# A landmark-attention decoder layer in f32: the column and row sums of the second attention move to GpSimd as trees of additions, the scale of its inverse is worked out over batches 1 to 4, and two softmax divisions are moved

## The chip, the core and the metric

The kernel runs on one core of one Trainium2 chip. A core has TensorE (matrix products, written PE in the profile; its weight loads are PEld), VectorE (DVE), ScalarE (ACT), GpSimd (POOL) and SyncE (SP), which issues most of the transfers. Each engine works through its own list of instructions in order, and they wait for one another by semaphores alone. The metric is the device time of one execution in microseconds. The kernel before takes 201.53 us, the median of three runs (200.58 to 201.87).

## The reference, cut to what matters

Eight batches of 128 tokens with 128 features go through landmark attention with 16 heads, an attention over a context, and a layer of experts, each followed by a layer norm. All of it is in f32. The change touches the first of the three:

```python
q_l = q.reshape(b, H, M, l, DH).sum(axis=3) / l      # M = 32 landmarks, l = 4, scale = DH ** -0.5
k_l = k.reshape(b, H, M, l, DH).sum(axis=3) / l
attn1 = softmax(q   @ k_l^T)      # 128 x 32 for each of 8 x 16 heads
attn2 = softmax(q_l @ k_l^T)      # 32 x 32
attn3 = softmax(q_l @ k^T)        # 32 x 128
z = attn2^T / (max(attn2.sum(-1)) * max(attn2.sum(-2)))   # both maxima over all batches and heads
for _ in range(6):
    az = attn2 @ z
    z = 0.25 * z @ (13 * I - az @ (15 * I - az @ (7 * I - az)))
out = attn1 @ z @ (attn3 @ v)
out = out + conv(out)                                     # along the tokens, 13 taps
```

The factor 1 / (max * max) is one number for the whole input. It is what the iteration starts from, and so the first matrices of the iteration need it.

## The kernel before, in words

**Setup.** The weights are transposed, landmark queries and keys formed, and the second attention `A2` [128, 32 groups, 32] is computed. Its softmax ends on VectorE. For each of 16 heads TensorE then forms a landmark map from the keys' and queries' weights, and ScalarE (10 heads) and VectorE (6 heads, `GG_VECTOR`) copy it from PSUM to `GG`. VectorE also transposes `A2` in 32 x 32 blocks into `A2T`.

**The scale.** VectorE sums `A2` and `A2T` along their rows (L1084, L1086), takes the largest of each (L1088, L1089) and gives `peak_ready`. TensorE turns these columns into rows (`peaks`, L520), VectorE takes the maximum over them, multiplies and inverts (L1091 to L1096), TensorE spreads the result over the 128 partitions (`scale`, L526), and VectorE copies it out (L1118), which gives `c_ready`. GpSimd scales `A2` by it into `V` (L376). TensorE squares `A2T` in two halves (`squares`, L559), and ScalarE scales these into `V` too (`first_P`, L909).

**The batch loop.** TensorE, VectorE, ScalarE and GpSimd each run through steps s = 0, 1, ... in an order written out by hand; later stages of a batch come some steps after its first. For batch s TensorE makes the scores of the first attention (L612) and of the third (L619). VectorE takes the maxima (L1106, L1109), subtracts the first (L1112) and scales the second (L1114). ScalarE does the exponentials: `A1` in one instruction (L921), `E3` in four (L924), with their sums. One step later VectorE sums `A1` and inverts both sums (L1128 to L1132), and GpSimd multiplies `E3` and `A1` by the inverses (L381, L384). Three steps later TensorE transposes `E3` (L645) and VectorE copies it (L1124); after four, TensorE multiplies by the tokens (L652) and ScalarE copies (`YT`, L918); after five, TensorE multiplies by the values' maps `NV` (L661), and ScalarE copies the result `R` (L937), which lies in the place of `E3`.

Other work is set in between, by the step s at which it stands in each engine's list: on TensorE `peaks` and `scale` at s = 0, the small transposes of the context and of a bias (L546 to L552) at s = 0, `squares(0)` at 1, the second half of the values' maps (`head_values(1)`, L534) at 2, `squares(1)` at 3. ScalarE copies the results of the small transposes after its exponentials of batch 0 (L896 to L903), and those of `head_values(1)` after batch 1 (L889, L891). VectorE begins batch 1 by an addition that waits for one of these copies (L1101, `gsum_ready`).

**The rest.** TensorE then runs the convolution of the first attention (L593), the 24 products of the iteration (L564, L570, in a hardware loop of 8 turns), with VectorE (L1147 to L1164) and ScalarE (L949) in turns with it, the product of inverse and `R` (L703), the output projection, and after that the second and third part of the layer.

The code below is printed with the profile's line numbers.

## Time and profile before

| | us |
|---|---|
| median of 3 runs (lowest, highest) | 201.53 (200.58, 201.87) |
| the profiled execution: its own time | 203.06 |
| span from its first to its last instruction | 201.3 |
| TensorE busy | 175.7 (87%) |
| VectorE busy | 123.8 (61%) |
| ScalarE busy | 97.0 (48%) |
| GpSimd busy | 68.7 (34%) |
| granted TensorE clock, mean | 0.975 of full |

The span is in the trace's own time, and the profiled execution was 1.8 us longer than it, and 1.5 us longer than the median run. TensorE's busy time is modelled from pipelined instructions, so that a stretch in which it is fully busy says that work stood ready, and not that the array ran at its peak. A shares-of-the-span table mixes stages with different limits; the stage of this change lies between 24 and 83 us.

### The profile page before, as it was taken

The numbers are of one execution on the slowest core, as the hardware profiler recorded it, in microseconds if no ns is written. First come the engines' busy times: TensorE is split into PE (matmuls) and PEld (weight loads), VectorE is DVE, ScalarE is ACT, GpSimd is POOL, SyncE is SP. The second block draws the span as 40 slices with busy tenths as digits, with TensorE's granted clock in tenths as the row PEclk, the third lists the DMA queues.
The fourth block names the chain that finished last, engine by engine and source line by source line (L and its number), as shares of the span: only waits on it lengthen the run. The fifth ranks groups of instructions, "written<-read, shape, count | busy, mean of one in ns | idle before, by whom it ended". The sixth has DMA issues, their size and how long they took to land. (4 is left out here: it accounts for less than half of the span.)

```text
span 201.3 us, 11917 instructions
## 1 busy us (share of the span) xinstructions
PE 175.7 (87%) x5244; PEld 153.5 (76%) x5244; DVE 123.8 (61%) x363; ACT 97.0 (48%) x264; POOL 68.7 (34%) x129
## 2 busy tenths in 40 slices
PE   0998996999999999739999999999899969899940
PEld 0986884767666769639899888999799759899940
DVE  0232798499998280235899893242579803988881
ACT  2422882569787446412343343322245617566750
POOL 6180000557565300000000001810226740689884
PEclk9999999999999999985999999999999999999996
DMA  5944000000000000000000000005960858787300
GB/s 178 373 125 141 7 0 0 0 10 3 0 3 0 3 3 7 3 3 3 0 0 0 2 2 0 7 3 165 352 101 26 250 144 224 200 215 234 97 8 4
DMA packets 15632, 14.57 MB, mean 72 GB/s; under 512 B 1350, under 2 KB 12001, under 8 KB 15603
## 3 DMA queue, kind: packets, MB, share of 16 engines
q1 hardware_dynamic: 14867, 13.10, 23.1%
q0 software_dynamic: 736, 1.06, 1.5%
q8 instruction: 21, 0.34, 0.7%
q14 instruction: 8, 0.07, 0.1%
HBM read 12.08 MB, written 2.53 MB: 73 GB/s over the span
## 5 line engine op out<-in xcount | busy, mean ns | idle before, releaser
L564 PE MATMUL banks<-V 32*32 32x64 f32 x1664 | 37.6, 231 | 6.0 <-issue 4.3
L564 PEld LDWEIGHTS banks<-V 32*32 32x32 f32 x1664 | 33.7, 107 | 8.6 <-issue 7.9
L570 PE MATMUL banks<-MM,WT 32*32 32x64 f32 x1536 | 35.8, 233 | 0.0
L570 PEld LDWEIGHTS banks<-MM,WT 32*32 32x32 f32 x1536 | 30.8, 107 | 0.0
L1154 DVE SCALAR_TENSOR_TENSOR MM<-V,banks 128x512 f32<-128x512 f32 x24 | 16.5, 686 | 18.1 <-PE banks L564 17.6
L949 ACT ACTIVATE V<-banks 128x512 f32<-128x512 f32 x20 | 11.9, 597 | 24.4 <-PE banks L570 24.4
L387 POOL MEMSET WT<- 128x1950 f32 x1 | 1.7, 1723 | 57.5 <-PE banks L570 57.5
L1019 ACT ACTIVATE GG<-banks,b1T 128x128 f32<-128x128 f32 x60 | 16.9, 378 | 5.6 <-PE banks L848 5.6
L848 PE MATMUL banks<-qkl,GG 128*128 128x128 f32 x120 | 15.9, 277 | 2.5 <-DVE qkl L1400 1.8
L848 PEld LDWEIGHTS banks<-qkl,GG 128*128 128x128 f32 x120 | 14.5, 192 | 3.1 <-DVE qkl L1400 2.0
L827 PE MATMUL banks<-E,GG 128*128 x120 | 16.3, 279 | 0.5 <-ACT GG L1019 0.5
L433 POOL DMA_INDIRECT out_x<-qkl,number_u x15 | 15.4, 1026 | 3.5 <-issue 3.5
L827 PEld LDWEIGHTS banks<-E,GG 128*128 128x128 f32 x120 | 14.6, 191 | 1.0 <-issue 0.7
L381 POOL TENSOR_TENSOR E<-E,st 128x512 f32<-128x512 f32 x8 | 8.3, 1043 | 10.2 <-DVE st L1128 10.2
L924 ACT ACTIVATE E<-banks,st 128x128 f32<-128x128 f32 x32 | 11.2, 368 | 0.0
L376 POOL TENSOR_SCALAR V<-A,st 128x512 f32<-128x512 f32 x2 | 3.1, 1594 | 23.3 <-DVE st L1118 23.3
L619 PEld LDWEIGHTS banks<-xT,GG 128*128 128x128 f32 x64 | 8.2, 191 | 3.7 <-issue 2.6
L661 PEld LDWEIGHTS banks<-NV,YT 128*32 128x32 f32 x256 | 6.6, 109 | 5.3 <-issue 5.3
L424 POOL TENSOR_TENSOR st<-st 128x1 f32<-128x1 f32 x13 | 7.6, 581 | 8.6 <-DVE st L1387 8.3
L1147 DVE SCALAR_TENSOR_TENSOR GB<-V,eye_a 128x256 f32<-128x256 f32 x24 | 10.0, 418 | 0.0
L1164 DVE TENSOR_TENSOR WT<-GB,banks 128x256 f32<-128x256 f32 x24 | 9.9, 414 | 0.0
L408 POOL DMA_INDIRECT sorted_tokens<-MM,slot_u x8 | 8.4, 1056 | 4.2 <-ACT MM L970 2.2
(217 smaller groups left out, 401.0 us busy)
## 6 DMA issues: line engine op xcount, KB each, us to landing
GG<-in_L_ffn_w SPq DMA_DIRECT2D x15, 256.0 KB
wqkv<-in_L_attn_w_qkv SPq DMA_DIRECT2D x3, 512.0 KB, 5.3
Tt<-padded_taps SPq DMA_DIRECT2D x1, 1024.0 KB, 5.7
sorted_tokens<-WT SPq DMA_DIRECT2D x1, 975.0 KB, 13.5
GG<-in_L_ffn_b SPq DMA_DIRECT2D x15, 64.0 KB
WT<-sorted_tokens SPq DMA_DIRECT2D x1, 585.0 KB, 4.6
x_sb<-in_x SPq DMA_DIRECT2D x1, 512.0 KB, 4.0
wfc<-in_L_attn_w_fc SPq DMA_DIRECT2D x1, 512.0 KB, 6.9
```

Of the source, the lines that this page charges most:

```text
L408: nc.gpsimd.indirect_dma_start(out=xs_dram.ap(), out_offset=bass.IndirectOffsetOnAxis(slot_u[:, b:b + 1], 0), in_=x2e[:, b, :], in_offset= ...
L433: nc.gpsimd.indirect_dma_start(out=out.rearrange("b n d -> (b n) d"), out_offset=bass.IndirectOffsetOnAxis(number_u[:, j:j + 1], 0), in_=y ...
L564: return mm(bank[PV_BANKS[k % RING]][quad(q), 64 * n:64 * n + 64], V[quad(q), g, 0, :], V[quad(q), g], start=True, stop=True)
L570: return mm(bank[QM_BANKS[k % RING]][quad((q + 2) % 4), 64 * n:64 * n + 64], Q[quad(q), g, :], MM[quad(q), g], start=True, stop=True)
L827: i = mm(bank[4 + j % 2][:, 0:D], hT[:, j % 3, P * k:P * k + P], w2s[:, experts[j], k, :], start=(k == 0), stop=(k == FK - 1))
L848: i = mm(bank[s % 3][:, P * k:P * k + P], w1b[:, s % W1_SLOTS, P * k:P * k + P], xsT[:, s, :], start=True, stop=True)
L924: nc.scalar.activation(E3[:, s, g, :], bank[5 + s % 2][:, N * g:N * g + N], ACT.Exp, bias=stat("nm3", HG * s + g, 1), scale=DH ** -0.5 / L ...
L949: nc.scalar.mul(V[:, ring(k + CH)], ps, 0.25).then_inc(V_ready, 1)
L1019: nc.scalar.activation(hT[:, j % 3, P * k:P * k + P], bank[j % 3][:, P * k:P * k + P], ACT.Gelu, bias=b1T3[:, experts[j], k:k + 1]).then_i ...
L1147: step(v.scalar_tensor_tensor(out=GB[:, g], in0=V[:, g, 0, :], scalar=QB, in1=eye_a[:].unsqueeze(1).broadcast_to([P, GC, M]), op0=ALU.mult ...
L1154: v.scalar_tensor_tensor(out=MM[:, g].rearrange("p g w m -> p (g w m)"), in0=V[:, g].rearrange("p g w m -> p (g w m)"), scalar=ROOT, in1=p ...
L1164: v.tensor_tensor(Q[:, g, :], GB[:, g], pv[:].rearrange("p (g w m) -> p g w m", g=GC, w=2)[:, :, 0, :], ALU.add).then_inc(Q_ready, 1)
```

## The change

The sums of `A2` and `A2T` are made by GpSimd, each as a tree of five additions (widths 16, 8, 4, 2, 1) in `MM`, which is free at that time. `peaks` goes to step 2 of TensorE (1 of VectorE), `scale` to step 3 (2 and 3), `squares` to 3 and 4, both `first_P` to 4 of ScalarE, and the two scalings by GpSimd behind batches 3 and 4. VectorE stores its six landmark maps one after the other and transposes `A2` behind them. The landmark maps are stored times `SIM_SCALE`, so that the exponentials and the maximum need no factor. The third attention's division is made on `R` (`scaled_R`, eight instructions behind all batches) and not on `E3`, and both sums are inverted by one instruction. The part of the diff that carries this:

```diff
+            def sums(src, out):
+                width, terms, at = M // 2, src, 0
+                while width >= 1:
+                    total = scratch[:, at:at + GROUPS * width].rearrange("p (g m) -> p g m", g=GROUPS) if width > 1 else out
+                    add = nc.gpsimd.tensor_tensor(total, terms[:, :, 0:width], terms[:, :, width:2 * width], ALU.add)
+                    if width > 1:
+                        add.then_inc(half_sums, 1)
+                        sums_begun[0] += 1
+                        pool.wait_ge(half_sums, sums_begun[0])
+                    else:
+                        add.then_inc(sums_ready, 1)
+                    terms, at, width = total, at + GROUPS * width, width // 2
...
+            pool.wait_ge(A2_ready, 2)
+            sums(A2[:], stat("cs").unsqueeze(2))
+            pool.wait_ge(A2T_ready, 1)
+            pool.wait_ge(sums_ready, 1)
+            sums(A2T[:], stat("rows").unsqueeze(2))
...
+            def scaled_R(b):
+                pool.wait_ge(R_ready, b + 1)
+                nc.gpsimd.tensor_tensor(R[:, b], R[:, b], stat("sm", (HG + H) * b, HG).unsqueeze(2)
+                                        .broadcast_to([P, HG, N]), ALU.mult).then_inc(R_scaled, 1)
...
+                if b in (3, 4):
+                    first_W(b - 3)
+            for b in range(B):
+                scaled_R(b)
...
-                    if s == 0:
-                        peaks()
...
+                if s == 2:
+                    peaks()
+                if s == 3:
+                    scale()
                 if s == 0:
-                    scale()
                     pe.wait_ge(NV_ready, 1)
...
-                if s == 1:
-                    pe.wait_ge(A2T_ready, 1)
-                    pe.wait_ge(c_ready, 1)
-                    squares(0)
...
                 if s == 3:
+                    pe.wait_ge(b1T_ready, 1)
+                    pe.wait_ge(A2T_ready, 1)
                     pe.wait_ge(NV_ready, 2)
+                    squares(0)
+                if s == 4:
+                    pe.wait_ge(c_ready, 1)
                     squares(1)
-                    pe.wait_ge(b1T_ready, 1)
                 if 3 <= s < B + 3:
                     b = s - 3
-                    pe.wait_ge(attn3_ready, b + 1)
+                    pe.wait_ge(exp3_done, HG * (b + 1))
...
-                    if b < 2:
-                        pe.wait_ge(V_ready, 2 * (b + 1))
+                    if b == 0:
+                        pe.wait_ge(V_ready, CH)
...
-            pe.wait_ge(R_ready, B)
+            pe.wait_ge(R_scaled, B)
...
-                if s == 1:
+                if s == 2:
+                    head_values(1, 0, 4)
+                if s == 4:
                     first_P(0)
-                    head_values(1, 0, 4)
-                if s == 3:
                     first_P(1)
...
-            for h in (9, 11, 13, 15):
-                GG_copy(h)
-            step(v.tensor_reduce(stat("cs"), A2[:], AX_X, ALU.add))
-            dve.wait_ge(A2T_ready, 1)
-            step(v.tensor_reduce(stat("rows"), A2T[:], AX_X, ALU.add))
...
-                    step(v.tensor_reduce(stat("nm3", HG * s, HG),
-                                         bank[5 + s % 2][:].rearrange("p (g n) -> p g n", g=HG), AX_X, ALU.max))
+                    v.tensor_reduce(stat("nm3", HG * s, HG), bank[5 + s % 2][:].rearrange("p (g n) -> p g n", g=HG),
+                                    AX_X, ALU.max, negate=True).then_inc(max3_ready, 1)
...
-                    v.tensor_scalar(stat("nm3", HG * s, HG), stat("nm3", HG * s, HG), -DH ** -0.5 / L, None,
-                                    ALU.mult).then_inc(max3_ready, 1)
-                if s == 0:
+                if s == 1:
+                    peaks()
+                if s == 2:
+                    scale()
+                if s == 3:
                     dve.wait_ge(c_mm, 1)
...
-                    v.reciprocal(stat("r3", HG * b, HG), stat("s3", HG * b, HG)).then_inc(rsum3, 1)
                     dve.wait_ge(exp1_done, b + 1)
-                    step(v.tensor_reduce(stat("rs1", H * b, H), A1[:, b], AX_X, ALU.add))
+                    step(v.tensor_reduce(stat("sm", (HG + H) * b + HG, H), A1[:, b], AX_X, ALU.add))
```

How this stands in the engines' lists is shown at three places. Line numbers are each kernel's own. First TensorE, steps 2 and 3 of the kernel before (L534 is `head_values(1)`, L559 `squares`, L645 the first transpose of `E3`):

```order
L612 MATMUL banks<-GG,GB 128x512 [waits sim1_shift]
L619 MATMUL banks<-xT,GG 128x128 [waits exp3_done]
L619 MATMUL banks<-xT,GG 128x128 x3
L534 MATMUL banks<-wfc,WT 128x128 [waits ctxT_ready]
L534 MATMUL banks<-wfc,WT 128x128 x7
L612 MATMUL banks<-GG,GB 128x512 [waits sim1_shift]
L619 MATMUL banks<-xT,GG 128x128 [waits exp3_done]
L619 MATMUL banks<-xT,GG 128x128 x3
L559 MATMUL banks<-A2T 32x32 [waits NV_ready]
L559 MATMUL banks<-A2T 32x32 x63
L645 MATMUL banks<-ident,E 128x128 [waits attn3_ready,b1T_ready]
```

The same steps in the changed kernel (L549 is `peaks`, L563 `head_values(1)`, L555 `scale`, L588 `squares(0)`):

```order
L646 MATMUL banks<-xT,GG 128x128 [waits exp3_done]
L646 MATMUL banks<-xT,GG 128x128 x3
L549 MATMUL banks<-ident,st 1x128 [waits peak_ready]
L549 MATMUL banks<-ident,st 1x128
L563 MATMUL banks<-wfc,WT 128x128 [waits ctxT_ready]
L563 MATMUL banks<-wfc,WT 128x128 x7
L641 MATMUL banks<-GG,GB 128x512 [waits sim1_shift]
L646 MATMUL banks<-xT,GG 128x128 [waits exp3_done]
L646 MATMUL banks<-xT,GG 128x128 x3
L555 MATMUL banks<-st,ones 128x1 [waits cinv_ready,const_ready]
L588 MATMUL banks<-A2T 32x32 [waits NV_ready,A2T_ready,b1T_ready]
L588 MATMUL banks<-A2T 32x32 x63
```

`peaks` now stands ahead of `head_values(1)`, and `scale` and a first half of the squares ahead of the first transpose of `E3`; in the kernel before one half of the squares stood in step 1 already. Second, ScalarE from batch 1 on in the kernel before (L909 is `first_P`, L889 and L891 store `NV`):

```order
L921 ACTIVATE A<-A 128x512 [waits sim1_shift]
L924 ACTIVATE E,st<-banks,st 128x128 [waits max3_ready]
L924 ACTIVATE E,st<-banks,st 128x128 x3
L909 ACTIVATE V<-banks,st 128x16x32 [waits c_ready,P0_mm]
L889 COPY NV<-banks 128x4x128 [waits NV_mm]
L891 COPY NV<-banks 128x4x128
```

The same engine in the changed kernel from batch 2 on (L920, L922 store `NV`, L951 stores `YT`, L940 is `first_P`):

```order
L954 ACTIVATE A<-A 128x512 [waits sim1_shift]
L957 ACTIVATE E,st<-banks,st 128x128 [waits max3_ready]
L957 ACTIVATE E,st<-banks,st 128x128 x3
L920 COPY NV<-banks 128x4x128 [waits NV_mm]
L922 COPY NV<-banks 128x4x128
L954 ACTIVATE A<-A 128x512 [waits sim1_shift]
L957 ACTIVATE E,st<-banks,st 128x128 [waits max3_ready]
L957 ACTIVATE E,st<-banks,st 128x128 x3
L951 COPY YT<-banks 128x512 [waits YT_mm]
L954 ACTIVATE A<-A 128x512 [waits sim1_shift]
L957 ACTIVATE E,st<-banks,st 128x128 [waits max3_ready]
L957 ACTIVATE E,st<-banks,st 128x128 x3
L940 ACTIVATE V<-banks,st 128x16x32 [waits c_ready,P0_mm] x2
```

The storing of `NV` stands behind the exponentials of batch 2 and no longer behind those of batch 1, and both `first_P` behind those of batch 4. Third, GpSimd between its first additions and the batches, in the changed kernel; none of these ten rows is in the kernel before, where the two scalings by the factor stood here:

```order
L380 TENSOR_TENSOR MM<-A 128x512
L380 TENSOR_TENSOR MM<-MM 128x256
L380 TENSOR_TENSOR MM<-MM 128x128
L380 TENSOR_TENSOR MM<-MM 128x64
L380 TENSOR_TENSOR st<-MM 128x32
L380 TENSOR_TENSOR MM<-A2T 128x512
L380 TENSOR_TENSOR MM<-MM 128x256
L380 TENSOR_TENSOR MM<-MM 128x128
L380 TENSOR_TENSOR MM<-MM 128x64
L380 TENSOR_TENSOR st<-MM 128x32
```

## Rows read from the trace of the kernel before

**Rows 1.** A stretch: start:end us, length, busy us (instructions) by engine, clock, DMA share, GB/s.

```profile
50.00:55.00 5.00, 5.00 (x51) 3.14 (x50) 4.90 (x13) 3.85 (x14) 2.90 (x3) 1.00 0.00 0
```

**Rows 2.** Instructions of TensorE in time: start us, duration us, what, idle before it.

```profile
30.71 1.16 PE L534 MATMUL banks<-wfc,WT 64*128 64x128 f32 x16 [0.71 <-DVE GG L1074]
...
32.12 1.07 PE L612 MATMUL banks<-GG,GB 128*128 128x512 f32 x2
...
45.86 1.29 PE L559 MATMUL banks<-A2T 32*32 32x32 f32 x128 [0.38 <-ACT NV L891]
47.08 0.66 PE L645 MATMUL banks<-ident,E 128*128 128x128 f32 x4
47.57 1.02 PE L612 MATMUL banks<-GG,GB 128*128 128x512 f32 x2
48.43 1.05 PE L619 MATMUL banks<-xT,GG 128*128 128x128 f32 x8
```

**Rows 3.** Waits of TensorE, 24 to 84 us: total, times, longest.

```profile
PE banks L520 <- DVE st L1089: 1.2, 1, 1.2
```

**Rows 4.** Instructions of ScalarE in time.

```profile
37.51 0.63 ACT L921 ACTIVATE A<-A 128x512 f32<-128x512 f32 x1 [4.21 <-DVE A L1112]
...
39.87 0.22 ACT L902 ACTIVATE res<-banks 128x8 f32<-128x8 f32 x1
...
42.24 0.63 ACT L921 ACTIVATE A<-A 128x512 f32<-128x512 f32 x1 [2.08 <-DVE A L1112]
...
44.15 0.69 ACT L909 ACTIVATE V<-banks,st 128x512 f32<-128x512 f32 x1
...
45.18 0.62 ACT L891 COPY NV<-banks 128x512 f32<-128x512 f32 x1
```

**Rows 5.** Instructions of VectorE in time.

```profile
31.68 1.20 DVE L1084 TENSOR_REDUCE st<-A 128x32 f32<-128x1024 f32 x1
...
40.12 0.17 DVE L1101 TENSOR_TENSOR res<-res,gw 128x8 f32<-128x8 f32 x1 [2.50 <-ACT res L902]
40.20 0.68 DVE L1106 TENSOR_REDUCE st<-banks 128x16 f32<-128x512 f32 x1
...
42.13 0.16 DVE L1114 TENSOR_SCALAR st<-st 128x4 f32<-128x4 f32 x1
...
43.14 0.63 DVE L1106 TENSOR_REDUCE st<-banks 128x16 f32<-128x512 f32 x1
...
49.49 0.63 DVE L1106 TENSOR_REDUCE st<-banks 128x16 f32<-128x512 f32 x1
...
52.97 0.63 DVE L1106 TENSOR_REDUCE st<-banks 128x16 f32<-128x512 f32 x1
```

**Rows 6.** Groups of GpSimd by shape: busy us, mean ns of one, idle before.

```profile
L384 POOL TENSOR_TENSOR A<-A,st 128x512 f32<-128x512 f32 x8 | 8.4, 1050 | 0.0
L376 POOL TENSOR_SCALAR V<-A,st 128x512 f32<-128x512 f32 x2 | 3.1, 1594 | 23.3 <-DVE st L1118 23.3
L394 POOL TENSOR_SCALAR MM<-st 128x1 f32<-128x1 f32 x8 | 1.7, 210 | 0.6
```

**Rows 7.** Stretches around the start of the iteration, columns as in Rows 1.

```profile
85.00:88.00 3.00, 1.35 (x125) 1.32 (x127) 0.87 (x4) 0.11 (x2) 0.00 (x0) 1.00 0.00 0
88.00:92.00 4.00, 1.86 (x128) 1.66 (x116) 1.23 (x3) 0.58 (x1) 0.00 (x0) 0.61 0.03 8
92.00:96.00 4.00, 3.81 (x268) 3.61 (x257) 2.71 (x6) 1.19 (x2) 0.00 (x0) 0.54 0.00 0
```

**Rows 8.** VectorE in the iteration, one row of this line for each product.

```profile
92.16 0.69 DVE L1154 SCALAR_TENSOR_TENSOR MM<-V,banks 128x512 f32<-128x512 f32 x1 [2.93 <-PE banks L564]
...
94.39 0.69 DVE L1154 SCALAR_TENSOR_TENSOR MM<-V,banks 128x512 f32<-128x512 f32 x1 [0.88 <-PE banks L564]
...
99.20 0.69 DVE L1154 SCALAR_TENSOR_TENSOR MM<-V,banks 128x512 f32<-128x512 f32 x1 [0.38 <-PE banks L564]
...
103.76 0.69 DVE L1154 SCALAR_TENSOR_TENSOR MM<-V,banks 128x512 f32<-128x512 f32 x1 [0.39 <-PE banks L564]
```

More of the change, by code:

```diff
@@ L24 @@
 GROUPS = B * HG
+SIM_SCALE = DH ** -0.5 / L
 CH = 4
@@ L372, in _ @@
                                     ).then_inc(xb_ready, 1)
-            pool.wait_ge(c_ready, 1)
-            for n in range(2):
+            def sums(src, out):
[10 more added lines that the diff above has]
+                    terms, at, width = total, at + GROUPS * width, width // 2
@@ L558, in squares @@
                         t = A2T[quad(q), g, :]
-                        i = mm(bank[3 + n][quad(q), M * (g % 16):M * (g % 16) + M], t, t, start=True, stop=True)
+                        i = mm(bank[4 - n][quad(q), M * (g % 16):M * (g % 16) + M], t, t, start=True, stop=True)
                 i.then_inc(P0_mm, 1)
@@ L883, in _ @@
                 act.wait_ge(GG_mm, h + 1)
-                nc.scalar.copy(GG[:, :, :, h, :].rearrange("p b w m -> p w b m"),
-                bank[(4 + h) % 8][:].rearrange("p (w b m) -> p w b m", w=2, b=B)).then_inc(GG_scalar, 1)
+                nc.scalar.mul(GG[:, :, :, h, :].rearrange("p b w m -> p w b m"),
+                              bank[(4 + h) % 8][:].rearrange("p (w b m) -> p w b m", w=2, b=B), SIM_SCALE
+                              ).then_inc(GG_scalar, 1)
             def head_values(n, first, second):
@@ L1080, in _ @@
+            for h in GG_VECTOR:
+                GG_copy(h)
             dve.wait_ge(A2_ready, 2)
             v.transpose(A2T[:].rearrange("p g m -> p (g m)"), A2[:].rearrange("p g m -> p (g m)")).then_inc(A2T_ready, 1)
-            for h in (9, 11, 13, 15):
-                GG_copy(h)
-            step(v.tensor_reduce(stat("cs"), A2[:], AX_X, ALU.add))
-            dve.wait_ge(A2T_ready, 1)
-            step(v.tensor_reduce(stat("rows"), A2T[:], AX_X, ALU.add))
-            settle()
-            step(v.tensor_reduce(stat("peak", 0, 1), stat("cs"), AX_X, ALU.max))
@@ L1089, in _, with peaks @@
-            v.tensor_reduce(stat("peak", 1, 1), stat("rows"), AX_X, ALU.max).then_inc(peak_ready, 1)
-            dve.wait_ge(peak_mm, 1)
-            step(v.tensor_reduce(stat("pk")[0:1, :], bank[3][0:1, 0:256].rearrange("p (w n) -> p w n", w=2),
-                                 AX_X, ALU.max))
-            settle()
-            step(v.tensor_tensor(stat("prod")[0:1, :], stat("pk", 0, 1)[0:1, :], stat("pk", 1, 1)[0:1, :], ALU.mult))
-            settle()
-            v.reciprocal(stat("cinv")[0:1, :], stat("prod")[0:1, :]).then_inc(cinv_ready, 1)
+            def peaks():
+                dve.wait_ge(sums_ready, 2)
+                step(v.tensor_reduce(stat("peak", 0, 1), stat("cs"), AX_X, ALU.max))
+                settle()
+                v.tensor_reduce(stat("peak", 1, 1), stat("rows"), AX_X, ALU.max).then_inc(peak_ready, 1)
@@ new lines, in scale @@
+            def scale():
+                dve.wait_ge(peak_mm, 1)
+                step(v.tensor_reduce(stat("pk")[0:1, :], bank[3][0:1, 0:256].rearrange("p (w n) -> p w n", w=2),
+                                     AX_X, ALU.max))
+                settle()
+                step(v.tensor_tensor(stat("prod")[0:1, :], stat("pk", 0, 1)[0:1, :], stat("pk", 1, 1)[0:1, :], ALU.mult))
+                settle()
+                v.reciprocal(stat("cinv")[0:1, :], stat("prod")[0:1, :]).then_inc(cinv_ready, 1)
```

44 lines of the change are left out of this document (23 added, 21 removed).

## The prediction, written before the changed kernel ran

> **What bounds the kernel now.** I read the busy shares first. TensorE is busy in 175.7 of 201.3 us, but that is an average over stages, so the stage of the change is read by stretches. From 50 to 55 us TensorE is busy in all 5.00 us and VectorE in 4.90 [rows 1]. Both look full, and the list in time tells them apart: VectorE begins a batch every 52.97 - 49.49 = 3.48 us [rows 5], and from batch 5 on TensorE has more than that to do for each. Between the first scores at 32.12 us [rows 2] and the end of the convolution at 82.6 us, TensorE stands still at few places: 1.2 us before `peaks` [rows 3], 0.38 us before `squares(1)` [rows 2], and pauses of weight loads around `scale` and the scores of batch 3 that I put at 0.1 and 0.6 us. Everything else there is work, and the changed kernel does the same work. So the end of this stage is: the time at which the first scores start, plus the same work, plus the pauses. From there on nothing is moved but one wait, and the rest of the kernel should shift as a whole. The question is only which pauses go and which come.
>
> **The start of the stage.** VectorE no longer transposes `A2` between its landmark maps, so the maps that `head_values(0)` waits for are stored 1.15 us sooner. The pause of 0.71 us before it [rows 2] goes; the pause has no more than this in it, since TensorE's own map products end then. What stands between it and the first scores takes 32.12 - 30.71 = 1.41 us of issue. First scores: 30.00 + 1.41 = 31.41 us, **0.7 us sooner**. The last map and the moved transpose (1.2 us, as for one L1084 [rows 5]) are through at 31.9, before the scores end at 32.5. Storing the maps with a factor is taken at the price of the copies; a map costs VectorE some 0.61 us of issue, and it has some 0.7 us to spare there, so up to a tenth more on each of six would cost nothing.
>
> **Batch 0.** `peaks` and `scale` are gone from step 0, with their 1.2 and 0.1 us. The scores of the third attention follow 0.86 us behind those of the first (48.43 - 47.57 [rows 2]) and end 1.05 us later, at 33.3. VectorE needs 0.64 us for the maximum, no longer waits for its end before subtracting (0.1 us a batch), and the subtraction of 0.69 us ends at 34.7. ScalarE starts its exponentials at 34.7 where it started at 37.51 [rows 4]: 2.8 us sooner. From there to the end of the copy that VectorE waits for is 39.87 + 0.22 - 37.51 = 2.58 us [rows 4], unchanged. VectorE begins batch 1 at 37.4 where it began at 40.20 [rows 5], again 2.8 us sooner. TensorE meanwhile does the small transposes and the scores of batches 1 and 2, and is through with them at 38.0, as the pitches of the same work give it (small transposes 1.14, scores 0.86 + 0.92 a batch).
>
> **First new pause, 1.6 us.** `peaks` stands behind those scores and waits for VectorE's two small maxima, which stand behind batch 1's three instructions. These took 42.13 - 40.20 = 1.93 us [rows 5], now 0.1 less: 37.4 + 1.8 = 39.2, plus some 0.4 for the small ones. TensorE stands from 38.0 to 39.6.
>
> **Second new pause, 2.1 us.** TensorE then does `peaks`, `head_values(1)` (1.09), and batch 3's scores, to 42.9, and `scale` for which VectorE is ready at 43.0. Next come `squares(0)`, and their list has a wait for `NV`, as bank 4 is shared. ScalarE stores `NV` behind the exponentials of batch 2. VectorE begins batch 2 at 39.6 + 0.86 - 0.1 = 40.4 (sum and inverse as between 42.13 and 43.14, less 0.15 for the two small instructions removed [rows 5]), so the subtraction ends at 42.25. The exponentials take 44.15 - 42.24 = 1.91 us, and storing `NV` takes 45.18 + 0.62 - 44.15 = 1.65 less the 0.57 of `first_P`, 1.08 [rows 4]. `NV` is stored at 45.3. TensorE stands from 43.2 to 45.3.
>
> **Where that leaves TensorE.** In the kernel before it started the second half of the squares at 45.86, with the first half done. Now it starts the first half at 45.3, with the second ahead. A half costs 47.08 - 45.86 = 1.22 us [rows 2]: -0.55 + 1.22 = **+0.7 us**.
>
> **Third new pause, 0.7 us.** The first product with `NV` (L661) now waits for both `first_P`, which ScalarE has behind batch 4's exponentials, and these behind the storing of `YT`. The product by the tokens ends at 51.4; then 0.48 + 1.91 + 1.27 = 3.66 us on ScalarE give 55.1. TensorE would be free at 54.4. So another **+0.7**, together **+1.4 us**.
>
> **What is covered.** The two trees: 992 elements each. At the nearest row of two inputs, 1050 ns for 512 [rows 6], 2.0 us, and with 0.2 us for the start of each of five and as much for each wait on itself, 3.6; from below 2.0, from above, at the slowest row (1594 ns for 512) with both, 5.1. The first may start at 27.05, when `A2` is ready, the second at 31.9, and `peaks` wants them at 39.2. Up to 6.0 us a tree nothing comes of it. The two scalings of 1.6 us are wanted some 20 us after they end. The eight multiplications of `R`, 1.04 us each, end some 1.1 us after the last `R`, near 79 us, and are wanted at 126. The multiplications of `E3` held nobody. On VectorE 0.27 us a batch is saved (two small instructions and the wait for the maximum), from batch 4 on under TensorE's work: nothing. Should those be worth their full 8 x 0.27 = 2.2 us, see the first rival.
>
> **The sum.** +1.4 us on the profiled execution, whose span would be 202.7; against the median run, 201.53 + 1.4 = **202.9**. The profiled execution was 1.5 us above that median, so its successor's own time says little alone. The start of the stage is surest within 0.3 us, the pauses within 0.4: +0.7 to +2.1. That is no change: a measurement tells about 1% (2.0 us) from none. Chance **0.48**.
>
> **Rival 1: VectorE paces the batches, and the kernel is faster.** For it: VectorE is at 4.90 of 5.00 us, batch 1 begins 2.8 us sooner, and 0.27 us a batch is removed. If the pauses I lay out were shorter, because ScalarE's and VectorE's pieces overlap more than the rows show, all of the 2.8 us would reach the end: 198.7. Against it: TensorE is at 5.00 of 5.00 [rows 1], and the three pauses hang on the order of the lists, which is fixed. With the loop entry below going well in addition it could also come out just under. Chance 0.13, of which 0.1 below -1%.
>
> **Rival 2: TensorE's clock falls in the new pauses, and the kernel is slower.** In the kernel before TensorE was busy in 1.35 of 3 us from 85 to 88, and then the granted clock fell to one half, 1.2 of 2.4 GHz: means of 0.61 and 0.54 over 8 us are some 6.8 us at the lower level [rows 7]. There the pauses before the fall were of 1.9 and 2.1 us. In the changed kernel TensorE would be busy in some 3.7 of the 7.3 us from 38.0 to 45.3, much the same picture, where before it was full. What it costs: a product of the iteration took 94.39 - 92.16 = 2.23 us at the lower level and (103.76 - 99.20) / 3 = 1.52 at the full [rows 8], so a third of the time is lost. Over 6.8 us that is 2.2 us, over half that long, as TensorE has work at hand at once here, 1.1; the whole +2.5 to +3.6, 204.0 to 205.1. It decides from the first fall after 43 us. Chance 0.28.
>
> The Trainium skill, in "TensorE: Matmul & The Clock Gate", section "Why this matters for your kernels", ties a fall to one long pause between bursts of products. By that rule neither of the new pauses would bring a fall, this rival would have next to no chance, and the sum would stay at +1.4. The trace disagrees: the fall at 88.9 us had only two short pauses ahead of it, with work between them [rows 7]. So the row decides, and the chance stays.
>
> **Rival 3: the trees are late.** Short runs of 16, 8, 4 elements may cost GpSimd more than a row of 512 shows. The trace has no such shape. At 7 us a tree, `peaks` comes 1.9 us later and everything behind it: +3.3, 204.8. Chance 0.05.
>
> **Rival 4: the loop's entry comes out otherwise.** From 82.5 to 96 us, where TensorE first runs through the loop's body, it loses some 5 us to pauses without a visible cause and to the lower clock. I let it shift as it stands. If the pauses or the clock fall otherwise, the whole moves by up to 1.6 us either way. Chance 0.06, and it widens each case.
>
> **The numbers.** The forecast's own range with the entry's noise is 201.4 to 204.0. Taking in rival 2 and the near edge of rival 1: 201.0 to 205.0, outside of it about 2 in 10. Slower by over 1%: 0.23 of rival 2, 0.05, 0.02 and 0.07 of the forecast's own upper end, 0.37. Faster by over 1%: 0.10 and 0.01, 0.11. The rest, 0.52, within 1%.
>
> **What would show it.** In the changed kernel's list: first scores near 31.4; ScalarE's first exponential near 34.7; a pause of TensorE before L549 ended by VectorE, near 1.6 us; one before L588 ended by `NV`, near 2.1; squares starting near 45.3; one before the first product with `NV`, ended by `V`, 0.7; the convolution ending near 84.0. GpSimd's second tree ends before 37. The granted clock is 1.00 throughout 38 to 60 us, or rival 2 holds. I am wrong if the convolution ends before 82.6, or if, ending near 84, it is made up for or doubled before 97.

## The result and the profile after

The changed kernel takes 207.83 us, the median of four runs (205.49 to 208.81); the kernel before took 201.16 beside it. The ratio, 1.025 with a 95% interval of 1.016 to 1.034, is made from the two quicker of these runs, and the profiled one isn't among them. So the kernel is slower by some 2.5%, where I forecast 0.7% and gave slower a chance of 0.37; the time is above my range.

| us, profiled executions | before | changed |
|---|---|---|
| own time, span | 203.06, 201.3 | 208.81, 206.9 |
| first scores after the first product of the landmark maps (22.27; 21.57) | 9.85 | 8.87 |
| **stage**: first scores to start of the convolution | 43.28 | 50.68 |
| convolution to first stored product of inverse and `R` | 51.94 | 52.13 |
| from there to the end | 73.96 | 73.65 |
| TensorE / VectorE / GpSimd busy | 175.7 / 123.8 / 68.7 | 178.8 / 122.5 / 75.1 |
| granted clock, mean | 0.975 | 0.952 |

That first product starts anywhere from 20.3 to 22.4 us in the 18 traces of this case, so I count from it. Everything lies in the stage: +7.40 us, of which an earlier start of 0.98 gives some back. The iteration's entry and all behind it shifted as a whole, as forecast.

The page of the changed kernel: busy time, and the granted clock in 40 slices.

```profile
PE 178.8 (86%) x5244; PEld 156.3 (76%) x5244; DVE 122.5 (59%) x345; ACT 96.9 (47%) x264; POOL 75.1 (36%) x139
...
PEclk9999999875799999996699999999999999999997
...
q8 instruction: 21, 0.34, 0.7%
```

TensorE's busy time rose by 3.1 us without more work, and the clock has a dip of three slices at 41 to 57 us (7, 5, 7) that it did not have. Now the waits of TensorE, 24 to 90 us (total, times, longest), where before only [rows 3] and the two short ones of [rows 2] stood:

```profile
PE banks L588 <- issue: 2.0, 1, 2.0
PE banks L549 <- DVE st L1120: 1.7, 1, 1.7
PE banks L691 <- ACT V L940: 0.8, 1, 0.8
PE banks L588 <- ACT NV L922: 0.4, 1, 0.4
```

The last three are the pauses that I laid out. The first I did not: it is "issue", a pause for nothing that the profile shows. Its place is seen in TensorE's list in time, in answer to [rows 2]:

```profile
30.44 1.07 PE L641 MATMUL banks<-GG,GB 128*128 128x512 f32 x2
...
35.93 1.06 PE L646 MATMUL banks<-xT,GG 128*128 128x128 f32 x8
38.70 0.38 PE L549 MATMUL banks<-ident,st 128*1 128x128 f32 x2 [1.70 <-DVE st L1120]
...
40.10 1.91 PE L641 MATMUL banks<-GG,GB 128*128 128x512 f32 x2
41.80 1.92 PE L646 MATMUL banks<-xT,GG 128*128 128x128 f32 x8
43.65 0.39 PE L555 MATMUL banks<-st,ones 1*128 1x1 f32 x2
44.44 1.26 PE L588 MATMUL banks<-A2T 32*32 32x32 f32 x127 [0.40 <-ACT NV L922]
47.72 0.21 PE L588 MATMUL banks<-A2T 32*32 32x32 f32 x1 [2.02 <-issue]
47.86 1.12 PE L675 MATMUL banks<-ident,E 128*128 128x128 f32 x4
48.77 1.91 PE L641 MATMUL banks<-GG,GB 128*128 128x512 f32 x2
50.47 1.91 PE L646 MATMUL banks<-xT,GG 128*128 128x128 f32 x8
52.32 1.86 PE L588 MATMUL banks<-A2T 32*32 32x32 f32 x128
54.11 0.66 PE L675 MATMUL banks<-ident,E 128*128 128x128 f32 x4
```

Two things are to be seen. `squares(0)` stops for 2.02 us between its 127th and its last record, with all of its operands there. (The trace has two matmul records for each f32 product, so 128 are its 64 products.) And the scores of batch 3 (from 40.10) and of batch 4 (from 48.77) take 1.7 and 1.85 us where they took 0.86 and 1.05 [rows 2]. The stretches show why (columns as in Rows 1):

```profile
38.00:40.00 2.00, 1.30 (x18) 1.06 (x18) 1.93 (x6) 1.64 (x8) 0.38 (x1) 1.00 0.01 4
40.00:42.00 2.00, 2.00 (x7) 0.87 (x4) 1.93 (x7) 1.07 (x5) 0.68 (x1) 0.57 0.00 0
...
44.00:46.00 2.00, 1.30 (x128) 1.20 (x128) 1.11 (x3) 1.22 (x5) 0.02 (x1) 1.00 0.03 8
46.00:48.00 2.00, 0.28 (x2) 0.14 (x2) 0.00 (x0) 1.10 (x7) 0.00 (x0) 0.78 0.00 0
48.00:50.00 2.00, 2.00 (x6) 1.44 (x7) 0.99 (x2) 0.00 (x0) 0.00 (x0) 0.50 0.03 8
```

The clock fell twice to its lower level, 1.2 of 2.4 GHz: from 40.3 to 43.7 us, 1.6 us behind the end of the pause before `peaks`, and from 47.1 to 54.0 us, from within the pause in the squares (45.7 to 47.7) on. In the kernel before it was 1.00 throughout 38 to 58 us. The last column, GB/s, shows 8 in the stretch in which the pause begins, and the queue that moves it is the instructions' own (q8 of the page): two transfers of 16 KB between 44 and 50 us, from 45.4 to 46.3 and from 49.3 to 50.3. So my new theory: **TensorE waits there for the next piece of its own program**, and the pauses bring the clock down.

The lists of the other engines answer to [rows 4, 5, 6]: ScalarE's first exponential, VectorE's first instruction of batch 1 and its small maxima, and the end of GpSimd's second tree.

```profile
33.76 0.63 ACT L954 ACTIVATE A<-A 128x512 f32<-128x512 f32 x1 [2.14 <-DVE A L1146]
```

```profile
36.37 0.17 DVE L1135 TENSOR_TENSOR res<-res,gw 128x8 f32<-128x8 f32 x1 [2.64 <-ACT res L933]
...
38.45 0.19 DVE L1120 TENSOR_REDUCE st<-st 128x1 f32<-128x32 f32 x1
```

```profile
31.26 1.28 POOL L380 TENSOR_TENSOR MM<-A2T 128x512 f32<-128x512 f32 x1 [1.51 <-DVE A2T L1114]
...
34.33 0.24 POOL L380 TENSOR_TENSOR st<-MM 128x32 f32<-128x32 f32 x1
```

A tree takes 3.3 us and the second ends at 34.6, 3.7 us before VectorE wants it at 38.25.

### The profile page after: what moved, and what is told of

It reads as the page before. It is cut to its first block and busy times, and to the rows that moved or that the text cites. A ratio compares the mean times of both kernels' runs of the same rounds, so it can differ in the third digit from the quotient of the medians.

```text
span 206.9 us, 11917 instructions
## 1 busy us (share of the span) xinstructions
PE 178.8 (86%) x5244; PEld 156.3 (76%) x5244; DVE 122.5 (59%) x345; ACT 96.9 (47%) x264; POOL 75.1 (36%) x139
## 3 DMA queue, kind: packets, MB, share of 16 engines
HBM read 12.08 MB, written 2.53 MB: 71 GB/s over the span
## 5 line engine op out<-in xcount | busy, mean ns | idle before, releaser
L409 POOL TENSOR_TENSOR A<-A,st 128x512 f32<-128x512 f32 x8 | 8.4, 1050 | 26.7 <-DVE st L1167 26.7
L646 PEld LDWEIGHTS banks<-xT,GG 128*128 128x128 f32 x64 | 10.1, 227 | 5.0 <-issue 3.9
L951 ACT COPY YT<-banks 128x512 f32<-128x512 f32 x8 | 4.8, 595 | 15.5 <-PE banks L682 15.5
L1182 DVE SCALAR_TENSOR_TENSOR GB<-V,eye_a 128x256 f32<-128x256 f32 x24 | 11.4, 473 | 0.0
L1160 DVE COPY E3T<-banks 128x512 f32<-128x512 f32 x8 | 5.5, 687 | 9.3 <-PE banks L675 9.2
L641 PE MATMUL banks<-GG,GB 128*128 128x512 f32 x16 | 10.2, 726 | 0.0
```

Source lines behind the costliest of these rows:

```text
L641: mm(bank[1 + s % 2][:], xTr[:, s, :], GG[:, s, 0].rearrange("p h m -> p (h m)"), start=True, stop=True).then_inc(sim1_mm, 1)
L1182: step(v.scalar_tensor_tensor(out=GB[:, g], in0=V[:, g, 0, :], scalar=QB, in1=eye_a[:].unsqueeze(1).broadcast_to([P, GC, M]), op0=ALU.mult ...
```

## The experiments

Times are medians (lowest, highest; runs), ratios are against the kernel before, run beside each group of experiments, with 95% intervals. "Stage" and "entry" are the third and fourth rows of the table above, in the one profiled execution of each kernel. The kernel before took 202.37, 202.35, 202.37 and 201.76 in the four groups (13 to 25 runs each).

**Do the divisions, the scaled maps and VectorE's shorter list do anything?** The kernel before, with these alone: the maps times `SIM_SCALE`, the negated maximum, one inverse for both sums, the division on `R`.

```diff
-                pool.wait_ge(rsum3, b + 1)
-                nc.gpsimd.tensor_tensor(E3[:, b], E3[:, b], stat("r3", HG * b, HG).unsqueeze(2)
...
+            for b in range(B):
+                pool.wait_ge(R_ready, b + 1)
+                nc.gpsimd.tensor_tensor(R[:, b], R[:, b], stat("sm", (HG + H) * b, HG).unsqueeze(2)
```

> The kernel before with the other half of the change alone: landmark maps stored scaled, negated maximum, third division on R by GpSimd, both sums inverted at once; no trees and no moved steps. Theory A (all of the loss is the moved steps): same as before within 0.5 us, as TensorE is full: 200.5 to 201.5 us. Theory B (the division on R or the scaled maps cost something): slower by 1 us or more. Theory C (VectorE paces the batches): faster by 1.5 us or more.

201.79 (200.71 to 202.61; 10), ratio 0.998 (0.993 to 1.003); stage 43.26 against 43.28. This half of the change is worth nothing: VectorE has 0.24 us less to do in a batch (it begins batch 2 2.64 us behind batch 1, where it was 2.88), and that reaches nobody. To this I added one step, the addition that waits for ScalarE (L1101 of before) in VectorE's step 2:

```diff
-                if s == 1:
+                if s == 2:
                     dve.wait_ge(gsum_ready, 1)
```

> e4 (the kernel before with the other half of the change) and VectorE's addition that waits for ScalarE moved from batch 1 to batch 2. Theory A (TensorE's work and its few waits set the stage): what can go is the waits of the scores of batch 3 and of NV, under 1 us: 200.5 to 202 us. Theory C (VectorE's start of batch 1 sets the pace): 2 us or more faster than before.

201.26 (199.68 to 202.64; 10), ratio 1.000 (0.994 to 1.006); stage 43.50. VectorE begins batch 1 6.1 us behind the first scores here and 8.1 in the kernel before, and TensorE is through no sooner, though two pauses by "issue" of 0.28 and 0.29 us hide up to 0.6 us of gain. So VectorE doesn't pace the batches.

**Is it the pauses?** The changed kernel, with products of no use set into its two longest laid-out pauses, so that TensorE stays busy:

```diff
                 if s == 2:
+                    fill(4, 7)
                     peaks()
...
                     scale()
+                    pe.wait_ge(b1T_ready, 1)
+                    fill(7, 8)
```

> The changed kernel with 7 idle 128-column products of TensorE ahead of the wait of peaks and 8 ahead of squares(0) (after the wait for b1T, in bank 7), results unused. Theory A (the excess over the laid-out +1.1 to +1.4 us is the lower clock that the two pauses bring on): granted clock 1.00 from 38 to 60 us, the scores of batch 3 back at 0.86 us of issue each, convolution some 4 us sooner than in the changed kernel, 202 to 204 us. Theory B (the excess is the pause inside squares(0) that nothing visible ends, and what follows it, whatever the clock does): that pause of 2.0 us stays, the time gains 1 us at most or none, 205 to 208.

207.55 (205.17 to 209.0; 4), ratio 1.022 (1.008 to 1.037). The stage falls from 50.68 to 46.08, with the clock at 1.00 from 38 to 58 us and, as I had not expected, without the 2.02 us of "issue" in the squares. But the entry grew from 52.13 to 53.44, and what lies behind it grew by 0.8; the profiled executions are 1.9 us apart, and the medians show nothing of it (207.55, 207.83). The filling changed two things at once: TensorE's activity, and where in its program everything behind stands (30 records further). The next kernels part these.

**The order of the waits.** `head_values(1)` again before `peaks` on TensorE and behind batch 1 on ScalarE, so that `NV` is stored early:

```diff
                 if s == 2:
+                    pe.wait_ge(ctxT_ready, 1)
+                    head_values(1, 0, 4)
                     peaks()
...
-                if s == 2:
+                if s == 1:
                     head_values(1, 0, 4)
```

> The changed kernel with head_values(1) ahead of peaks on TensorE and NV stored behind batch 1 on ScalarE, as in the kernel before. Theory A (order of the lists): the wait of squares(0) for NV goes (2.05 us), the wait of peaks falls from 1.7 to 0.6, laid out 0.9 us faster than before and 2 us faster than the laid-out change; with no long pauses the clock stays up, so 200 to 201.5 us. Theory B (unseen pause at the squares independent of both): still a 2 us pause within squares(0), 202 to 204.

204.57 (202.76 to 205.5; 4), ratio 1.011 (1.000 to 1.021); stage 46.15, the clock at 1.00. The wait for `NV` is gone, the one before `peaks` shrank to 0.6, and two of 0.5 came, before batch 3's scores and `scale`. The squares still stop at the same record:

```profile
43.01 1.27 PE L588 MATMUL banks<-A2T 32*32 32x32 f32 x127
46.48 0.18 PE L588 MATMUL banks<-A2T 32*32 32x32 f32 x1 [2.20 <-issue]
```

To this kernel I added `first_P(0)` on ScalarE one step earlier, and VectorE's addition one step later:

```diff
-                if s == 4:
+                if s == 3:
                     first_P(0)
+                if s == 4:
                     first_P(1)
...
-                if s == 1:
+                if s == 2:
                     dve.wait_ge(gsum_ready, 1)
```

> As e2, and VectorE's addition that waits for ScalarE's small copies is moved from batch 1 to batch 2, and first_P(0) from batch 4 to batch 3 of ScalarE. Theory A: VectorE starts batch 1 some 2.5 us sooner, laid out 3.1 us faster than before: 197.5 to 199.5 us. Theory B (VectorE's early start is given back, as TensorE is full from there on, or the unseen pause stays): no better than e2 by over 0.5 us.

203.32 (202.26 to 204.55; 10), ratio 1.008 (1.003 to 1.014); stage 44.83. The waits for other engines are down to 0.3 and 0.2 us. The stop of 1.55 us in the squares is still there, and behind it the clock falls to 0.57 from 44 to 48 us. The waits that I laid out are real, and each goes when its cause goes.

**The trees.** The kernel with `head_values(1)` back, but the sums made by VectorE in its wait before batch 1:

```diff
-            sums(A2[:], stat("cs").unsqueeze(2))
...
-            sums(A2T[:], stat("rows").unsqueeze(2))
...
                 if s == 1:
+                    v.tensor_reduce(stat("cs"), A2[:], AX_X, ALU.add).then_inc(sums_ready, 1)
+                    dve.wait_ge(A2T_ready, 1)
+                    v.tensor_reduce(stat("rows"), A2T[:], AX_X, ALU.add).then_inc(sums_ready, 1)
                     dve.wait_ge(gsum_ready, 1)
```

> e2 with both sums made by VectorE as in the kernel before (2 x 1.2 us), put where it waits for ScalarE ahead of batch 1; no trees. Theory A (the trees are covered and buy nothing, as VectorE has 2.6 us free just there): stage as e2 (46.15 us) within 0.3, 204 to 205 us. Theory D (the trees free VectorE): 1 us or more slower than e2.

205.58 (202.74 to 205.66; 6), ratio 1.016 (1.009 to 1.024); stage 46.09 against 46.15 with trees. VectorE's list:

```profile
34.14 1.21 DVE L1125 TENSOR_REDUCE st<-A 128x32 f32<-128x1024 f32 x1
35.27 1.21 DVE L1127 TENSOR_REDUCE st<-A2T 128x32 f32<-128x1024 f32 x1
36.87 0.17 DVE L1130 TENSOR_TENSOR res<-res,gw 128x8 f32<-128x8 f32 x1 [0.39 <-ACT res L925]
```

In the changed kernel it stood still there for 2.64 us anyway, so the trees move work into GpSimd that costs the stage nothing on VectorE. (The whole, 1.016 against 1.011 for the kernel with trees, is not told apart: the intervals overlap.)

**The pause in the squares: their pace, or their place in the program?** First their pace. A half of the squares is 64 tiny products, 128 records and as many weight loads in 1.2 us. Here each half is parted in two, with the scores or other products between:

```diff
-            def squares(n):
+            def squares(n, lo=0, hi=16):
...
+                    if s == 4:
+                        squares(0, 8, 16)
...
-                    squares(0)
+                    squares(0, 0, 8)
```

> The changed kernel with each half of the squares in two pieces of 32 products, with scores, transposes or the product by the tokens between the pieces; same work, same waits. Theory A (the pause of 2.0 us in squares(0) is TensorE's next 16 KB of program coming too late, because 64 tiny products pass one such piece in 1.2 us): the pause goes, what is left of it under 0.5 us; the waits for peaks (1.7) and NV and the clock's falls stay; some 2 us faster than the changed kernel, about 205 us. Theory B (the pause belongs to the place, a wait that the profile does not show): a pause of 2 us stays somewhere between 44 and 50 us and the time is that of the changed kernel within 0.5 us.

206.57 (206.02 to 207.56; 4), ratio 1.025 (1.016 to 1.035); stage 48.32, 2.4 us less than in the changed kernel. The ratio is that of the changed kernel all the same, so the gain that I expected of the whole did not show. There are two shorter stops in place of one, longer than the 0.5 us that I had allowed, and the rows between them can be counted:

```profile
46.62 0.69 PE L588 MATMUL banks<-A2T 32*32 32x32 f32 x57
48.05 0.26 PE L588 MATMUL banks<-A2T 32*32 32x32 f32 x7 [0.74 <-issue]
48.23 1.16 PE L649 MATMUL banks<-xT,GG 128*128 128x128 f32 x8
49.32 0.75 PE L588 MATMUL banks<-A2T 32*32 32x32 f32 x64
50.01 0.66 PE L678 MATMUL banks<-ident,E 128*128 128x128 f32 x4
50.59 0.59 PE L588 MATMUL banks<-A2T 32*32 32x32 f32 x45
51.89 0.37 PE L588 MATMUL banks<-A2T 32*32 32x32 f32 x19 [0.71 <-issue]
```

From stop to stop: 7 + 8 + 64 + 4 + 45 = 128 products' records, each with its weight load: 256 instructions for one transfer of 16 KB. The Trainium skill, in "Advanced Engine Details and Errata", section "ISA Cache", gives 16 KB and 256 instructions as one line; the count agrees.

The same split on the two better orders:

> e2 (NV back behind batch 1) with the squares in pieces as in e5. Theory A: e2's pause of 2.2 us goes, clock 1.00 throughout the stage, so e2 minus 2 us, 201.5 to 203 us, no slower than before. Theory B: same as e2 within 0.5 us, 204 to 205.

203.68 (201.65 to 205.44; 10), ratio 1.006 (1.000 to 1.012); stage 45.91, stops of 0.65 and 0.44 us.

> e3 (NV back, VectorE's addition at batch 2, first_P(0) at batch 3) with the squares in pieces. Theory A: e3's pause of 1.55 us and its fall of the clock after it go, some 3 us off e3, 199 to 201 us, faster than before by 1 to 3 us. Theory B: same as e3, 202.5 to 204.

201.42 (199.91 to 207.48; 10), ratio 0.999 (0.993 to 1.004); stage 42.99, one stop of 0.44 us. With the order mended and the squares parted, the change has cost nothing. In both the clock stays at 1.00 from 38 to 58 us.

Then their place. Eight tiny products of no use, 16 records, in step 1 of the kernel with `head_values(1)` back; the squares stay whole and merely stand 16 records further down:

```diff
+                if s == 1:
+                    pe.wait_ge(A2T_ready, 1)
+                    for q in range(8):
+                        t = A2T[quad(q % 4), 0, :]
+                        mm(bank[4][quad(q % 4), 0:M], t, t, start=True, stop=True)
```

> e2 and, in step 1 of TensorE, 8 more tiny products (32x32x32, results unused, 0.15 us together, a pause stands behind them anyway). They show as 16 more matmul records ahead of squares(0), an eighth of the 128 that lie between two unexplained pauses. Theory A (the program comes in pieces of 128 matmuls with their loads, the next is asked for when one is begun and is there some 3.4 us later; squares(0) is just one such piece): the piece now begins 16 records sooner, ahead of two waits and some 4 us before the end of squares(0); the pause of 2.2 us goes, under 0.3 left; the stage from first scores to convolution 44 us (e2: 46.15). Theory B (the place, or the number of tiny products in a row, makes the pause): still 2 us within squares(0), stage 46 us.

202.18 (201.25 to 203.88; 10), ratio 1.003 (0.998 to 1.008); stage 44.79, 1.4 us less than without (46.15). The stop of 2.20 us is gone, and one of 0.77 us has come some 25 us further down, among the tiny first products of the iteration:

```profile
41.12 1.29 PE L588 MATMUL banks<-A2T 32*32 32x32 f32 x128
```

The changed kernel itself with 16 such products:

> The changed kernel itself and 16 such tiny products in step 1. Theory A: the pause of 2.0 us in squares(0) goes, and with it the second fall of the clock; the wait for peaks, the first fall and the last wait stay; stage 46.5 to 48 us (changed kernel: 50.68, e5: 48.3), 204 to 206 us. Theory B: stage 50 us or more, 206 to 208.

205.92 (204.18 to 208.76; 4); stage 46.04. Neither the stop nor a fall of the clock is there (I had expected the first fall to stay), and so this stage is the changed kernel's as I had forecast it. Its list:

```profile
37.81 0.38 PE L549 MATMUL banks<-ident,st 128*1 128x128 f32 x2 [1.13 <-DVE st L1125]
...
39.22 1.13 PE L641 MATMUL banks<-GG,GB 128*128 128x512 f32 x2
...
41.23 0.35 PE L555 MATMUL banks<-st,ones 1*128 1x1 f32 x2
43.56 1.28 PE L588 MATMUL banks<-A2T 32*32 32x32 f32 x128 [1.98 <-ACT NV L927]
44.77 0.66 PE L680 MATMUL banks<-ident,E 128*128 128x128 f32 x4
...
48.44 0.66 PE L680 MATMUL banks<-ident,E 128*128 128x128 f32 x4
...
53.80 1.08 PE L696 MATMUL banks<-NV,YT 128*32 128x128 f32 x32 [0.80 <-ACT V L945]
```

Start and stage together are 1.8 us over the kernel before, and the entry takes 53.26 us here, 1.3 more; that is most of what it is slower. So what the shift gave back in the stage it partly lost at the entry.

**Can the kernel before be given the pause?** Its order unchanged, with 8 and with 32 such products ahead of `squares(0)`:

```diff
                     pe.wait_ge(A2T_ready, 1)
+                    for q in range(32):
+                        t = A2T[quad(q % 4), 0, :]
+                        mm(bank[4][quad(q % 4), 0:M], t, t, start=True, stop=True)
```

> The kernel before and 8 tiny products ahead of squares(0), 16 matmul records. Open so far: the kernel before passes the same 64 products of squares(1) without the pause that the changed kernel has. Theory A1 (only where the borders of the 128-record pieces fall counts, and before they fall well): a pause may appear or not in the squares, and those at the loop's entry move by 16 records; the stage 43.4 us plus whatever pause appears. Theory A2 (a piece is asked for early enough unless TensorE has stood still before it): no pause in the stage wherever the borders fall, stage 43.3 to 43.6 us.

> As e13 with 32 tiny products, 64 records, half a piece; 0.6 us of work more. Theory A1: a pause of 1 us or more in one of the halves of the squares, if the borders before fell well; at the loop's entry the pauses move by half a piece. Theory A2: no pause in the stage, 43.8 to 44.2 us.

With 8: 202.39 (one run), stage 44.30. The squares run through, but there is a stop further down, among the first products of the iteration, which the kernel before passes without one; with it, the stage is 1.0 us longer:

```profile
69.45 0.35 PE L564 MATMUL banks<-V 32*32 32x64 f32 x9 [0.78 <-issue]
```

With 32: 214.28 (one run), stage 47.46, and

```profile
39.33 1.01 PE L559 MATMUL banks<-A2T 32*32 32x32 f32 x98
42.87 0.44 PE L559 MATMUL banks<-A2T 32*32 32x32 f32 x28 [2.53 <-issue]
```

with the clock at 0.59 and 0.55 in the two stretches of 2 us behind it. The pause and the fall come to the kernel before, by nothing but 64 records more. (Of its 214.28 us, 6 lie far behind this stage, where the clock was at its lower level for 20 us.)

**How exact is the place?** The best order (as e3 above), whole squares, with 4, 8 and 16 products of no use.

> As e15 with 4, 8 records. Theory A: the pause in the squares is gone or under 0.5 us (its piece now holds scale, its wait and half of the last scores), the entry as in e3 or e9: 199 to 201 us. Theory B: as e10, 202 to 203.

204.42 (202.02 to 204.55; 4), ratio 1.010 (1.001 to 1.020); stage 46.46. The stop moved from behind the 127th record to behind the 119th, by just the 8 records put ahead, but it didn't get shorter, against what I expected of the theory; one of 0.92 us stands among the first products of the iteration:

```profile
41.20 1.20 PE L588 MATMUL banks<-A2T 32*32 32x32 f32 x119
44.65 0.33 PE L588 MATMUL banks<-A2T 32*32 32x32 f32 x9 [2.24 <-issue]
```

> e10 with 8 tiny products in place of 16. e10 was 2.3 us sooner at the convolution than the kernel before, and lost 2.0 at the entry of the iteration's loop. Theory A (both come from where the program's pieces begin): with 8, as in e9, the pause in the squares is gone all the same and the entry costs what it did in e9 (convolution to first stored product of R 51.8 us, e10 53.4): stage 41.9, 199 to 201 us, faster than before by 1 to 2 us. Theory B (the entry's loss comes from the stage being through sooner): 53 us or more from convolution on, 202 to 203 us.

200.47 (198.55 to 206.01; 11), ratio 0.992 (0.987 to 0.997): the fastest version, and faster than the kernel before by some 0.8%. (Its profiled execution, 206.01 us, had the clock at its lower level for 20 us far behind the entry, so its stages are used and its whole is not.) Stage 43.04, where I had expected 41.9: a stop of 0.30 us in the second half of the squares and one of 0.77 in the first products of the iteration. Entry 51.86.

> e3 and 16 such tiny products in step 1. Theory A: e3's pause of 1.55 us goes, and the fall of the clock after it; stage 41.5 to 42.5 us (e3: 44.83, before: 43.28), some 2 us faster than before with the sooner start, 199 to 201 us. Theory B: as e3, 203.

202.73 (200.75 to 205.13; 10), ratio 1.001 (0.995 to 1.007). Stage 41.97, the shortest of all, 1.3 us less than before and started 1.0 us sooner; but entry 53.44. TensorE's waits from 72 to 96 us in this kernel:

```profile
PE banks L593 <- issue: 6.0, 3, 2.3
```

and in the one with 8 products:

```profile
PE banks L593 <- issue: 3.9, 2, 2.2
```

So the entry's pauses "without a visible cause" also hang on the place, and a shift that clears one stage can load the other. The kernels with the long entry (53.1 to 53.4 us: e1, e10, e11 and e14) have one more stop of 1.4 to 1.8 us there, and the clock at its lower level for 10.2 us; all others have 6.8 us of it, and 50.7 to 52.1.

**What all 18 traces say together.** Two counts over the traces tie the stops to the program. First their place: counted from TensorE's first product, every stop in the squares stands behind the 600th or the 728th record (the 601st in e14), and every one in the first products of the iteration behind the 1104th, whatever lies there (one more, of 0.29 us in e8, behind the 1102nd); the stops of the entry stand 127 records apart. In the kernel before, the 601st record is the last one ahead of `squares(1)`, where TensorE waits 0.38 us for `NV` anyway. So shifting moves the code past the places, and not the places. Second their end: all 61 pauses over 0.25 us for which TensorE waited for no engine, in the stage and at the entry, end 1.2 to 1.6 us behind the end of a transfer of 16 KB by the instruction queue. In the changed kernel that transfer began at 45.4 us, with the squares already running, and there was none of 16 KB in the 20 us before; in e11 one came in the stretch from 35 to 37 us, long before the squares:

```profile
35.00:37.00 2.00, 1.68 (x10) 1.05 (x8) 1.52 (x4) 0.52 (x4) 0.00 (x0) 1.00 0.03 8
```

It is the same in e9, e10 and e15 (35.8 to 36.5 us), where no stop stands behind the 600th record; in e16, as in e2, e3 and e12, none came between 26 and 41.9 us, and the stop stands.

## Why the prediction was wrong

| step | forecast | measured |
|---|---|---|
| first scores sooner | 0.7 | 0.98 |
| ScalarE's first exponential, behind the first map product | 12.4 (34.7) | 12.2 (33.76) |
| pause before `peaks` | 1.6 | 1.70; 1.13 in e11 |
| pause before `squares(0)`, for `NV` | 2.1 | 0.40; 1.98 in e11 |
| pause before the first product with `NV` | 0.7 | 0.80 |
| these together, against before | +1.4 | +1.8 (e11: 46.04 - 43.28 - 0.98) |
| a tree | 3.6 | 3.3 |
| stop in the squares for instructions | not in the sum | 2.02 |
| clock | falls with chance 0.28, costs 1.1 to 2.2 | fell twice, 2.6 net |

**The waits were right.** The order of the lists gave the three pauses, their releasers and nearly their lengths. In the changed kernel the pause for `NV` was only 0.40, because at the lower clock the scores ahead of it took 43.65 - 40.10 = 3.55 us where e11 took 41.23 - 39.22 = 2.01. The 1.54 lost there were taken from a wait of 1.98: the first fall cost next to nothing. (The 3.6 us for a tree doesn't come out of its own terms: 2.0 and five starts and five waits of 0.2 make 4.0. Measured were 3.3, and nothing hung on it.)

**The step that failed** is the sentence "Everything else there is work, and the changed kernel does the same work. So the end of this stage is: the time at which the first scores start, plus the same work, plus the pauses." It counts as pauses only waits for other engines. TensorE can also wait for its own instructions, and the same squares that ran through in the kernel before stopped for 2.02 us at their 127th record. I had such pauses before my eyes, in rival 4, and kept them to the loop's entry, where "I let it shift as it stands"; that they hang on where the code stands, and so on every edit ahead, I did not ask. Shown by: e9 and e11 (the stop goes with the squares whole and 16 or 32 records more), e16 (it moves by exactly 8 records), e14 (it comes to the kernel before), and the two counts over all traces.

**Rival 2 was the right mechanism with too small a chance and price.** The fall after 38 us came at the first laid-out pause and cost little; the one that counts came in the stop that I didn't forecast. From the first transpose behind `squares(0)` to the one behind `squares(1)` the changed kernel took 54.11 - 47.86 = 6.25 us, e11 48.44 - 44.77 = 3.67: 2.58 us. That closes the account of the profiled execution: the stage is longer than e11's by 50.68 - 46.04 = 4.64, of which 2.02 are the stop and 2.58 the second fall. With the 1.8 of the waits it makes 6.4 us from the setup's end on. It is an account of that one execution: the other runs have no trace, and the ratio of 1.025 stands for some 5 us. But all four runs of the changed kernel had a mean clock of 0.952 to 0.959, and of 76 runs of the kernel before beside the experiments 74 had 0.963 to 0.977 (the other two 0.953 and 0.958), so a longer time at the lower level was not the profiled run's alone.

The Trainium skill's rule of one long idle stretch ("TensorE: Matmul & The Clock Gate", "Why this matters for your kernels"), against which I weighed this rival, would have forecast no fall; the two falls at pauses of 1.70 and 2.02 us speak against it here. Nor does a pause of that length decide: e11 kept its clock over 1.13 and 1.98 us, e12 over 1.87, e2 over 2.20, while e3 lost it at 1.55, e16 at 2.24 and e14 at 2.53. What tells them apart, these profiles don't settle.

**Rival 1** (VectorE paces) fell with e4 and e8. **Rival 3** (late trees) fell with the trace. What I called covered (both trees, the scalings, the division on `R`, VectorE's 0.27 us a batch, of which 0.24 came) was: e4's stage is the same within 0.02 us, e12's within 0.06.

**Still open:** when the next piece of the program is asked for. The places of the borders can be counted from a trace, but not whether TensorE will stop there: with 8 records more ahead of the squares (e16) the transfer still came at 42.0 us and the stop was as long as before, with 16 (e15) it came at 36.0 and the stop was gone; and the second half of the squares, as dense as the first, never stopped for more than 0.71 us in any profile.

## What to carry to other kernels

When an edit adds, removes or moves instructions on an engine, look for dense stretches of tiny instructions behind it and read the pauses ended by "issue" in the trace of before: they may go or come with the edit, at 0.3 to 2.5 us each here. Count the records between two of them, and look whether each ends just behind a transfer of the instruction queue. A few idle products ahead try out another place cheaply (here four changed nothing, and eight cleared the squares but let a stop of 0.8 us appear further down). Count what such a pause can do to the clock as well as the pause itself. And before moving work off an engine, look at what that engine waits for there: put into VectorE's wait (e12), the sums cost the stage nothing.

## What the runs showed of the hardware

- TensorE stopped at fixed places of its program, 128 products' records (256 instructions with the weight loads) apart in e5, and each stop ended 1.2 to 1.6 us behind a transfer of 16 KB by the instruction queue. A stop in the first half of the squares took 1.6 to 2.5 us where these ran 128 records in 1.2 us, without other products between (the changed kernel, e2, e3, e12, e14, e16), and a stop in either half 0.4 to 0.7 where other products were set between (e5 to e7).
- Additions of two inputs by GpSimd took 1290, 725, 458, 294 and 242 ns for 512, 256, 128, 64 and 32 elements a partition in runs of 16, 8, 4, 2 and 1, where a multiplication of 512 by factors that stand for 32 elements each took 1050 [rows 6].
- A lower clock in front of a wait for another engine cost next to nothing: 1.54 us of slower scores shortened a wait of 1.98 to 0.40.
